# The gathers of a ring buffer: the first pair of each half turn waits until every pair ahead of it has landed

## The reference, cut to what matters

```python
def _graph_conv_max(x, src, dst, W_rel, b, W_root):
    agg = jax.ops.segment_max(x[src], dst, num_segments=N)   # N = 1250
    agg = jnp.where(jnp.isfinite(agg), agg, 0.0)
    return agg @ W_rel.T + b + x @ W_root.T

h = jax.nn.relu(_graph_conv_max(x, src, dst, W1_rel, b1, W1_root))
h = jax.nn.relu(_graph_conv_max(h, src, dst, W2_rel, b2, W2_root))
```

## Time and profile before

| | |
|---|---|
| median of 3 runs | 944.09 us (943.99 to 945.03) |
| profiled execution: from first to last instruction | 1025.1 us |
| PE busy | 726.0 us (71%) |
| DVE busy | 681.6 us (66%) |
| ACT busy | 270.3 us (26%) |
| POOL busy | 546.7 us (53%) |
| granted TensorE clock, mean | 0.884 |
| chain that ended last | PE 33%, DVE 25%, issue 19%, POOL 3%, DMA 2% |

### The profile page before, as it was taken

How to read it: one execution, slowest core, us unless ns; L and a number is a source line. 1 busy time by engine, 2 the same in 40 slices (tenths; PEclk the granted TensorE clock), 3 DMA queues, 4 the chain that set the end, 5 groups by cost and what they waited for, 6 DMA issues and landing times.

```text
span 1025.1 us, 9702 instructions
## 1 busy us (share of the span) xinstructions
PE 726.0 (71%) x2541; PEld 329.5 (32%) x2541; DVE 681.6 (66%) x1232; ACT 270.3 (26%) x389; POOL 546.7 (53%) x537
## 2 busy tenths in 40 slices
PE   0317555778378778866488657887698678789996
PEld 0214222333133323322133323333243235344442
DVE  3768565588758767873888774898588879733120
ACT  0264250222022202222434030343243122012222
POOL 5652326557746675764556655566447200565644
PEclk9757877899789989987899878998899889899999
DMA  5715336557746675656657756666566400377656
GB/s 136 219 36 183 101 97 184 162 170 214 216 116 194 184 218 144 202 168 184 174 177 214 226 163 180 189 213 193 158 193 187 143 12 1 113 235 142 105 102 82
DMA packets 64770, 162.18 MB, mean 158 GB/s; under 512 B 16383, under 2 KB 20755, under 8 KB 64709
## 3 DMA queue, kind: packets, MB, share of 16 engines
q0 software_dynamic: 40448, 124.74, 44.6%
q1 hardware_dynamic: 17004, 17.16, 6.0%
q10 hardware_dynamic: 7272, 19.74, 5.9%
HBM read 143.37 MB, written 18.11 MB: 158 GB/s over the span
## 4 chain that ended last, share of the span: by engine, by line
PE 33%; DVE 25%; issue 19%; another core or an unknown queue 9%; ACT 5%; POOL 3%; DMA 2%; DVEq 2%; POOLq 0%; ACTq 0%; SPq 0%
PE pp L1165 8%; DVE acc L891 6%; PE prow L1136 5%; PE pp L1563 5%; DVE weights L902 5%; PE pp L1576 4%; PE prow L1103 3%; PE prow L1124 2%; DVE mem L1403 2%; POOL mem L838 1%; DMA mem<-tab,ic 1%; PE pp L1346 1%; PE prow L519 1%; PE pp L501 1%
## 5 line engine op out<-in xcount | busy, mean ns | idle before, releaser
L838 POOL DMA_INDIRECT mem<-tab,ic x372 | 389.5, 1047 | 266.9 <-issue 136.5
L1165 PE MATMUL pp<-weights,slots 128*128 128x512 bf16 x1200 | 306.8, 405 | 114.8 <-DVE acc L891 70.2
L891 DVE TENSOR_TENSOR acc<-acc,pp 128x1024 f32<-128x1024 f32 x180 | 219.1, 1217 | 85.3 <-PE pp L1165 33.5
L1165 PEld LDWEIGHTS pp<-weights,slots 128*128 128x128 bf16 x1200 | 118.0, 103 | 307.5 <-issue 103.8
L902 DVE TENSOR_TENSOR weights<-weights,mem 128x1024 f32<-128x1024 f32 x129 | 158.1, 1226 | 17.9 <-DVE weights L902 11.3
L1136 PE MATMUL prow<-weights,aggT 128*128 128x512 f32 x160 | 92.2, 708 | 37.4 <-ACT aggT L1213 20.5
L1124 PE MATMUL prow<-weights,rootT 128*128 128x512 f32 x160 | 76.0, 619 | 0.0
L1615 POOL DMA_INDIRECT out<-mem,node_of x28 | 44.2, 1577 | 47.3 <-ACT mem L1593 40.9
L1544 DVE COPY weights<-prow 128x512 f32<-128x512 f32 x28 | 18.7, 688 | 72.1 <-PE prow L1103 71.7
L1604 POOL DMA_INDIRECT mem<-xnd,slot_of x20 | 22.0, 1099 | 78.4 <-DVE weight_of L1538 72.6
L1213 ACT ACTIVATE aggT<-prow 128x512 f32<-128x512 f32 x20 | 11.9, 597 | 192.5 <-PE prow L1103 98.7
(11 more groups left out here) (349 smaller groups left out, 828.0 us busy)
## 6 DMA issues: line engine op xcount, KB each, us to landing
slots<-ttd ACTq DMA_DIRECT2D x20, 640.0 KB
mem<-tab,ic POOLq DMA_INDIRECT x372
weights<-in_L_ffn_W SPq DMA_DIRECT2D x9, 512.0 KB, 5.1
weights<-in_L_ffn_W ACTq DMA_DIRECT2D x7, 512.0 KB
xnd<-xin ACTq DMA_DIRECT2D x10, 256.0 KB
mem<-in_x SPq DMA_DIRECT2D x2, 1120.0 KB
tab<-mem SPq DMA_DIRECT2D x1, 2240.0 KB
weights<-in_L_gnn_W_rel SPq DMA_DIRECT2D x2, 1024.0 KB
```

The costliest lines, as they stand in the source:

```text
L838: g.indirect_dma_start(ring[:, h * PAIR + k, :], None, tables[l], bass.IndirectOffsetOnAxis(ic[:, j * PAIR + k:j * PAIR + k + 1], 0))\
L891: v.tensor_tensor(acc[:, :, :], acc[:, :, :], pp[j % 2][:, :, :], ALU.max).then_inc(S["pa"], 1)
L1165: ins = t.matmul(pp[j % 2][:, i, :], sel[u][:, j * KP + i, :], hot[:, j, w, :], start=w == 0, stop=w == 2)
```

## The change

One line in `gathers` changes. For `h == 0` the threshold at `ready` goes from `j + 1` to `j + FLYING`: since `ready` starts at `FLYING`, this lets the pair go only when all pairs ahead of it have landed. All other pairs wait as before. There are 16 half turns in each layer.

```diff
                 g.wait_ge(S["done"], base_g + i * LAP + (j + 1))
                 g.sem_inc(S["apart_g"], 1)
-                g.wait_ge(S["ready"], base_g + i * LAP + (j + 1))
+                g.wait_ge(S["ready"], base_g + i * LAP + (j + FLYING if h == 0 else j + 1))
                 g.sem_inc(S["apart_g"], 1)
                 if h == 0:
                     g.wait_ge(s_ic[l][b], i * 16 + 16)
```

## The result

The changed kernel took 1001.95 us (median of 4 runs, 1000.49 to 1002.66) beside 944.48 us of the kernel before (4 runs, 943.99 to 945.03): ratio 1.0617, 95% interval 1.0588 to 1.0647, or 57.5 us more. It is slower, as forecast, but three times as much as forecast (57.5 us against 18.6), and beyond the range.

What follows compares the result with a forecast made beforehand. The prediction took POOL's gather supply as close to the bound, busy at least 0.76 of the time, binding in the heavy tile. Its terms, 9.3 + 1.8 + 5.5 + 2 = 18.6 us, on 944.1 gave 962.7, predicted 963 us, range 948 to 978.

Steps and rivals of the forecast that it cites:

- the price at a quick landing: At a gate behind a busy POOL queue: waiting for a landing of 3.60 us costs 3.24 us.
- POOL waits 108.8 us with a full ring anyhow, so most of it can be hidden: Over all 30 gates: their full price of 97 us mostly fits into POOL's existing waits for slots.
- term 4: From profiled execution to median: with fewer stalls the ring is less full, one more heavy-tile gate may come through; +2 us.
- Heavy tile of layer 0: Pairs 24 to 37: three gates with no idle time to hide them, less 0.4 us of slack; +9.3 us.
- Heavy tile of layer 1: Pairs 117 to 130: POOL's 9.51 us wait pays the first two gates, the third is paid; +1.8 us.
- Term 3: Tiles that begin right behind a gate: 2.9 us at one, 1.3 at each of two more; +5.5 us.
- The supply becomes the bound: Rival, gather stages: ring nearly always empty, every tile of nine or more pairs pays; about 40 us, 984; chance 0.14.
- gates are hidden while there is spare time: Rival, whole kernel: gates hidden but for the heavy tile; 4 to 7 us, 949 us; chance 0.27.
- Faster: Rival, DMA path: the emptied queue removes long gathers, heavy tiles lose 3 to 5 us of them; 940 us; chance 0.04.
- near 80 us in some 27: POOL at every sixth pair: idle about 3.5 us each until SyncE's line 805, near 80 us in some 27 waits.
- up by about the time lost: DVE's waits for landings at line 805: up from 15.9 us by about the time the kernel loses.
- Ordinary tiles lose as well as the heavy ones: Sign of being wrong, in the gather stages: ordinary tiles also get longer; no size given.

Runs made afterwards that it cites:

- e9: The unchanged kernel before, profiled again among undisturbed runs; 943.92 us.
- e7: The changed kernel with the second gather of each pair left out and VectorE taking the first row twice; 933.29 us, ratio 0.9895 to the kernel before.
- e12: Kernel before plus a gate at each half turn that leaves one pair in flight, undisturbed; 947.21 us, ratio 1.0042.
- e1: The unchanged kernel before, profiled once more in a disturbed set of runs; 1032.19 us.
- e4: Kernel before plus a gate at each half turn that leaves one pair in flight, in a disturbed set; ratio 0.9769.
- e16: Kernel before with no gate and two pairs in flight in place of three, in a disturbed set; ratio 0.9770.
- e2: Kernel before plus the gate only at the first half turn of each lap, in a disturbed set; 1056.51 us.
- e3: Kernel before plus the gate in layer 0 only, in a disturbed set; ratio 1.0042.
- e13: Kernel before plus the gate at the fourth pair of each half turn in place of the first, in a disturbed set; ratio 0.9974.
- e14: Kernel before plus the gate in layer 1 only, in a disturbed set; ratio 1.0162.
- e8: Kernel before plus the gate at every pair; 1511.58 us, ratio 1.6023.

## Why the prediction was wrong

- **Right: the mechanism, its direction, and the price at a quick landing.** The gate holds POOL from the landing of the last pair, 3.32 us in the chain against 3.24 forecast. All gates of the trace together are 114.7 us, not 97, because 3.60 us was one quick landing taken for all; the tail up to 10.2 us was not in the sum. Once the spare time is spent each us of a gate is a us of the stage, so this is some 17 us of the 39 missing.
- **Wrong: the step "POOL waits 108.8 us with a full ring anyhow, so most of it can be hidden".** The trace was of a disturbed execution, and its slack was taken for that of the timed runs. Undisturbed, POOL waits 38.3 us for slots, and in all about 62 us of the gather stages were free, where the trace read has 132. So of 97 us of gates 35 could not be hidden even at the prediction's own price, and of the measured 114.7 us 53 could not. The prediction also set 501 us of supply against 656 us, the pause between the layers included; undisturbed that stretch is 592.9 us, a share of 0.85 in place of 0.76, and without the pause (567.3 us, with e9's 507.5 us of supply) it is 0.89.
- **Wrong: term 4.** It named the difference, 81 us between profile and median, and knew that stalls fill the ring, and then put +2 us on it. Subtracting the 81 us from the stage would have left 575 us for 598 us of supply with gates, so +23 as the least; with 3.8 us a gate, +40. The question that the prediction asked, where the ring is empty, was the right one; the trace could not answer it.
- **Terms 1 to 3.** Heavy tile of layer 0: +9.3 forecast, +13.6 measured (36.4 to 50.0). Heavy tile of layer 1: +1.8 forecast, +9.3 measured (38.6 to 47.9): the wait of 9.51 us that was to pay for its first two gates stood in a tile that lasted 44.8 us in the trace read. Term 3 had three tiles and 5.5 us, and nothing for the other twenty or so gates because "POOL catches up"; 11 of 16 ordinary tiles lose, those of layer 0 26 us in all.
- **The rivals.** "The supply becomes the bound" is what happened: POOL waits for slots 1.5 us in 5 waits. It was given 0.14 and priced at about 40 us, because the spare time and the price of a gate were those of the trace read. That gates are hidden while there is spare time is what e7 and e12 show, for a cheaper supply and a softer gate. "Faster" had no part: the mean gather is 1,071 ns after and 1,064 in e9.
- **What the profile after was to show.** POOL's waits at line 805 "near 80 us in some 27": 128.4 in 65, of which 32.8 in 42 were there in e9 already. DVE's waits "up by about the time lost": from 28.4 us (17.6 + 6.0 + 4.8) to 95.4 on the same lines, 67 for 58 lost. "Ordinary tiles lose as well as the heavy ones" was named as a sign of being wrong, and it came. The other sign, idle times at the gates below 2 us, did not: the least is 3.0.

## What to carry to other kernels

A wait added to a producer costs what it holds less what the producer can spare, stage by stage, and nothing until that is spent. Count the spare time as the length of the stage less the producer's operations with the gaps between them, and take the stage length from an execution that is as long as the runs that are timed: here a profile 8.6% longer than the median showed 132 us of slack where the timed runs have 62. For the price of a wait on a landing take the spread of the landings, not one.

## What was not expected of the hardware

The same kernel took 939 to 948 us in four sets of runs and 1018 to 1061 us in two others, on two chips that showed both at different times. The disturbed traces hold single late starts of instructions that wait for TensorE; ScalarE's copies at lines 1208 and 1213 start up to 7.3 us late in e1 and up to 10.8 in the trace of before, and 0.04 us late in e9 but for the first. These account for some 46 and 49 us, if each is counted in full. What causes them is open. In the two disturbed sets e4 and e16 (two pairs in flight) were each 2.3% faster than the kernel before, though they have the same transfers; but the other versions that hold gathers back (e2, e3, e13, e14) were not, so that fewer gathers in flight help is not shown. The granted clock was lower where TensorE was idle more: 0.95 and 0.94 in the gather stages of e9, where it is busy for 0.81 and 0.78 of the time, and 0.73 and 0.74 in those of e8, where it is for 0.49 and 0.50.
